# Row 1 of the input and two constant matrices are loaded in 32 by 32 blocks and turned by DVE instead of TensorE

## The reference

```python
rw = softmax(cond_8); w, sel = top_k(rw, 2); w = w / w.sum(-1)     # 8 x 8 logits
# layer 0: two routed experts of eight for each row, and one shared expert
mlp(x, g, u, d) = (gelu(x @ g) * (x @ u)) @ d                      # 256 -> 1024 -> 256
x = x + sum_of_two(w_e * mlp(x, expert_e)) + mlp(x, shared)
# layer 1: a base matrix, and LoRA over 8 experts of rank 16
out  = x @ W_base.T + b_base
lora = einsum('bter,eor,be->bto', x @ As.T, Bs, cond_8)
x = x + out + lora * 2
```

## Time and profile before

| | us |
|---|---|
| median of 3 runs | 806.5 (806.18 to 807.17) |
| the profiled execution | 806.55 |
| its span in the profile | 804.7 |
| outside the span | 1.85 |
| PE busy | 795.9 (99% of the span) |
| DVE busy | 692.3 (86%) |
| ACT busy | 472.3 (59%) |
| POOL busy | 241.2 (30%) |

### The profile page before, as it was taken

The page is one execution under the profiler, slowest core; times in us unless marked ns, Lnnn a source line. Parts: engine busy times, 40 slices in busy tenths (PEclk is TensorE's granted clock), DMA queues, the critical chain, the costliest instruction groups (busy, mean ns, idle before and its releaser), DMA issues.

```text
span 804.7 us, 13013 instructions
## 1 busy us (share of the span) xinstructions
PE 795.9 (99%) x4014; PEld 678.6 (84%) x4014; DVE 692.3 (86%) x896; ACT 472.3 (59%) x715; POOL 241.2 (30%) x218
## 2 busy tenths in 40 slices
PE   9999999999999999999999999999999999999998
PEld 7888888888888888789888889878888887898887
DVE  4886987987876899899989989998898998999886
ACT  5574564554644566476556567556656665765563
POOL 1441321321110443322532412342242332226220
PEclk9999999999999999999999999999999999999999
DMA  7340520303213432353343335235324423623200
GB/s 201 82 118 13 148 76 15 117 1 103 94 40 91 146 118 79 105 157 96 124 140 89 101 119 167 86 104 130 107 96 159 110 79 104 168 96 126 69 1 27
DMA packets 120141, 80.56 MB, mean 100 GB/s; under 512 B 62480, under 2 KB 115472, under 8 KB 120080
## 3 DMA queue, kind: packets, MB, share of 16 engines
q1 hardware_dynamic: 120080, 79.88, 33.0%
HBM read 67.28 MB, written 12.58 MB: 99 GB/s over the span
## 4 chain that ended last, share of the span: by engine, by line
PE 69%; DVE 16%; issue 9%; ACT 2%; POOL 2%; DVEq 1%; DMA 0%; POOLq 0%; ACTq 0%
PE ps_ring L719 42%; PE ps_acc L719 25%; DVE inner_lo L1377 4%; DVE wide L1377 2%; DVE post L1636 2%; DVE post L1696 2%; DVE xc L1377 1%; ACT wide L1048 1%; POOL post L696 1%; DVE post L1611 1%; ACT post L1051 1%; DVE coef_now L1692 1%; DVE post L1654 1%; DVE post L1645 1%; PE ps_ring L839 1%
## 5 line engine op out<-in xcount | busy, mean ns | idle before, releaser
L719 PE MATMUL ps_ring<-xc,wide 128*128 128x512 f32 (+1 forms) x2076 | 454.2, 367 | 0.0
L719 PEld LDWEIGHTS ps_ring<-xc,wide 128*128 128x128 f32 x2076 | 366.3, 188 | 65.6 <-issue 0.2
L1048 ACT CAST inner_hi<-post 128x512 fp32r<-128x512 f32 x192 | 118.1, 623 | 169.6 <-DVE post L1696 87.7
L719 PE MATMUL ps_acc<-inner_hi,wide 128*128 128x512 f32 x504 | 172.9, 391 | 2.4 <-DVE post L1611 2.4
L1377 DVE TENSOR_TENSOR inner_lo<-post,inner_hi 128x512 fp32r<-128x512 f32 x192 | 164.4, 872 | 6.1 <-ACT inner_hi L1048 5.7
L696 POOL TENSOR_TENSOR post<-post 128x512 f32<-128x512 f32 x24 | 31.0, 1292 | 296.5 <-DVE post L1647 296.5
L719 PEld LDWEIGHTS ps_acc<-inner_hi,wide 128*128 128x128 f32 x504 | 94.7, 188 | 24.5 <-issue 4.6
L1051 ACT ACTIVATE post<-ps_ring 128x512 f32<-128x512 f32 (+1 forms) x132 | 73.3, 558 | 54.3 <-PE ps_ring L719 48.1
L719 PE MATMUL ps_acc<-inner_lo,wide 128*128 128x512 f32 x252 | 98.4, 390 | 0.0
L719 PE MATMUL ps_acc<-inner_hi,sh_dn 128*128 128x512 f32 x256 | 83.9, 389 | 0.0
L1696 DVE SCALAR_TENSOR_TENSOR post<-post,coef_now,ps_ring 128x512 f32<-128x512 f32 x80 | 59.5, 744 | 27.8 <-PE ps_ring L719 27.5
(11 more groups left out here) (122 smaller groups left out, 836.6 us busy)
## 6 DMA issues: line engine op xcount, KB each, us to landing
raw<-n_L_cond_skill_gate_dram SPq DMA_DIRECT2D x32, 256.0 KB, 2.7
raw<-in_L_cond_skill_up_dram SPq DMA_DIRECT2D x32, 256.0 KB, 3.3
raw<-n_L_cond_skill_down_dram SPq DMA_DIRECT2D x32, 256.0 KB, 3.7
xbuf<-n_L_cond_skill_gate_dram SPq DMA_DIRECT2D x32, 256.0 KB, 2.8
xbuf<-in_L_cond_skill_up_dram SPq DMA_DIRECT2D x32, 256.0 KB, 3.2
xbuf<-n_L_cond_skill_down_dram SPq DMA_DIRECT2D x32, 256.0 KB, 3.9
xt_scratch<-xbuf SPq DMA_DIRECT2D x8, 512.0 KB, 3.3
sh_scratch<-stage SPq DMA_DIRECT2D x8, 512.0 KB, 2.8
```

Of the source, the lines that this page charges most:

```text
L719: last = pe.matmul(dst, left_[a], right_[b], start=start and n == 0, stop=stop and n == len(PASSES) - 1, skip_group_check=adds)
L1048: return nc.scalar.copy(dst, src)
```

## The change

Row 1 of `x` is loaded in 8 block DMAs in place of one, turned by two DVE transposes straight into `xbuf` (a new semaphore `xt1_in`), and split from there. PE's 8 transposes of row 1 go, and so do ACT's two copies to `xbuf`. `w_base` comes in 8 block DMAs in place of one and B in 8 in place of two; DVE turns both into `w_id` and `b_t` where it copied them out of PSUM. `turn_constants` with its six PE transposes goes.

```diff
@@ SP
+            load_x_blocks(1, x_blk1)
-            sp.dma_start(x_nat1, x_rows[1]).then_inc(x_landed[1], 16)
             load_gate_up(1, sh_landed[1], sh_landed[1])
...
-            sp.wait_ge(turned, 4)
+            sp.wait_ge(xt1_in, 2)
             load_x_blocks(3, x_blk1)
...
+                    w_rows = w_base.rearrange("(k j) h -> j k h", j=32)
                     for c in range(HC):
-                        sp.dma_start(b_nat[:, c, :].rearrange("p (e r) -> p e r", e=E),
-                                     lora_b[:, c * P:(c + 1) * P, :].rearrange("e p r -> p e r"))\
-                            .then_inc(layer1_landed, 16)
-                    sp.dma_start(w_nat, w_base.rearrange("(c p) h -> p c h", p=P))\
-                        .then_inc(layer1_landed, 16)
+                        for g in range(4):
+                            h0 = c * P + 32 * g
+                            sp.dma_start(w_blk[32 * g:32 * (g + 1), c * H:(c + 1) * H]
+                                         .rearrange("j (k i) -> j k i", i=32),
+                                         w_rows[:, :, h0:h0 + 32]).then_inc(layer1_landed, 16)
+                    b_cols = b_blk.rearrange("p (k f r) -> p f k r", f=2, r=R)
+                    for e in range(E):
+                        g, f = divmod(e, 2)
+                        sp.dma_start(b_cols[32 * g:32 * (g + 1), f],
+                                     lora_b[e].rearrange("(k j) r -> j k r", j=32)).then_inc(layer1_landed, 16)
                     store_shared(Q - 1)
@@ PE
-                pe.wait_ge(x_landed[1], 16)
-                for c in range(HC):
-                    turn(acc[1][c], x_nat1, c)
                 pe.wait_ge(left_ready, LEFT_BLOCKS[0])
...
-                    if k == CONST_STEP and first:
-                        pe.wait_ge(acc1_out, 2 * Q)
-                        turn_constants()
                     if k == FOLD_STEP:
                         if first:
-                            pe.wait_ge(w_turned, 1)
+                            pe.wait_ge(acc1_out, 2 * Q)
@@ ACT
             take_xt(0, acc[0][0])
+            act.wait_ge(xt1_in, 1)
+            split_right(0, B12, xt(1, 0))
             gelu_block(0, 0, 0)
+            act.wait_ge(xt1_in, 2)
+            split_right(0, B22, xt(1, 1))
             gelu_block(0, 2, 2)
-            act.wait_ge(turned, 3)
-            split_right(0, B12, acc[1][0][:])
-            act.wait_ge(turned, 4)
-            split_right(0, B22, acc[1][1][:])
             split_left(1)
...
             gelu_block(0, 3, 2)
-            take_xt(2, acc[1][0])
-            take_xt(3, acc[1][1])
@@ DVE
-            split_right(0, B12, acc[1][0][:], 3)
-            split_right(0, B22, acc[1][1][:], 4)
+            dve.wait_ge(x_landed[1], 128)
+            for c in range(HC):
+                V.transpose(xt(1, c), x_blk1[:, c, :]).then_inc(xt1_in, 1)
+            dve.wait_ge(xt1_in, 2)
+            split_right(0, B12, xt(1, 0), 3)
+            split_right(0, B22, xt(1, 1), 4)
...
-                dve.wait_ge(turned_w, 1)
-                V.tensor_copy(b_t[:], ps_misc[1][:, 0:H]).then_inc(b_t_done, 1)
-                V.tensor_copy(w_id[:], ps_misc[0][:]).then_inc(w_turned, 1)
+                dve.wait_ge(layer1_landed, (3 + 2 * E) * 16)
+                V.transpose(b_t[:], b_blk).then_inc(b_t_done, 1)
+                V.transpose(w_id[:], w_blk).then_inc(w_turned, 1)
```

More of the change, by code:

```diff
@@ L153, in cond_resid_kernel @@
         x_nat = xbuf[:, 4 * S:6 * S].rearrange("p (t h) -> p t h", t=TT)
-        x_nat1 = stage[:, 0, :].rearrange("p (t h) -> p t h", t=TT)
         x_blk = xbuf[:, 4 * S:6 * S].rearrange("p (c n) -> p c n", c=HC)
@@ L238, in cond_resid_kernel @@
         a_nat = post[:, 0:H]
-        b_nat = post[:, H:2 * H].rearrange("p (c n) -> p c n", c=HC)
-        w_nat = post[:, 2 * H:4 * H].rearrange("p (c h) -> p c h", c=HC)
+        b_blk = post[:, H:2 * H]
+        w_blk = post[:, 2 * H:4 * H]
         t_tmp = stage[:, 0, :]
@@ L270, in cond_resid_kernel @@
         sum_done = sem("sum_done")
-        turned_w = sem("turned_w")
         fold_done = sem("fold_done")
@@ L277, in cond_resid_kernel @@
         xt0_in = sem("xt0_in")
+        xt1_in = sem("xt1_in")
         right_hi = sem("right_hi")
@@ L441, in store_xt @@
                 if qn == 0:
-                    sp.wait_ge(xt0_in, 2 * r + 2)
+                    sp.wait_ge(xt0_in if r == 0 else xt1_in, 2)
                 else:
@@ L816, in shared_down_part @@
                 if u == 0 and p == 0:
-                    pe.wait_ge(xt0_in, 4)
+                    pe.wait_ge(xt0_in, 2)
                 if q > 0 and j == 0 and p == 0:
@@ L967, in layer1_last @@
                         one(t, 1, 1, 0, False, True).then_inc(l1_done, 1)
[L969 to L977, removed]
             def row(b, par, first):
@@ L1268, in ex_copy_out @@
                     if first:
-                        act.wait_ge(turned_w, 1)
+                        act.wait_ge(w_turned, 1)
                         act.wait_ge(a_ready, 1)
@@ L1354, in row @@
                     if first and k == CONST_STEP:
-                        act.wait_ge(layer1_landed, 6 * 16)
+                        act.wait_ge(layer1_landed, (3 + 2 * E) * 16)
                         take_hi(a_s[0], a_nat).then_inc(a_hi, 1)
@@ L1397, in turn_x @@
             def turn_x(qn, r):
-                dve.wait_ge(x_landed[r], 16 + 128 * qn)
+                dve.wait_ge(x_landed[r], (16 if r == 0 else 128) + 128 * qn)
                 if qn > 1:
```

## The result

| | before | after |
|---|---|---|
| median, us | 806.36 (8 runs, 806.1 to 807.17) | 809.15 (8 runs, 808.52 to 811.32) |
| ratio | | 1.0035 (95% interval 1.0026 to 1.0044) |
| the profiled execution / its span, us | 806.55 / 804.7 | 809.15 / 807.3 |

What follows compares the result with a forecast made beforehand. PE was taken to bound most stretches, but the store, POOL and DVE the second place. Terms -0.68 (start), +0.05 (DVE) and +0.05 (queue) sum to -0.58 us, from 806.55 to 806.0; range 804.9 to 808.3.

Steps and rivals of the forecast that it cites:

- Later SP gains: SP's queue after the start: row 3's blocks issued some 1.7 us earlier, DVE's wait shrinks, 0.10 us comes back.
- the freed wait: SP's second `xt` store no longer waits for ACT's last copy of row 1; through by about 17, not 18.79.
- The rival on the other side: Slower side: sixteen issues hold the shared-result stores back, up to 0.70 us each, 808.1 or more; chance 0.18.
- the second place: Last shared results, stores from about 260 us: PE's transposes worth nothing, DVE 0.05 and queue 0.05 us lost.
- The start's own sum: Start, row 1: 0.88 saved by PE's transposes, less 0.3 stall, plus 0.1 from row 3's blocks, 0.68 us gained.
- The 13.02 of the forecast: Start: when PE asks for all of row 1, from 10.30 plus 12 matmuls of 2.72 us.
- The stall: Start: PE waits some 0.3 us near 13 for row 1's second low part; bounds none to 1.3 us.
- the forecast's 9.85: Start: landing of row 1's blocks, last issue at 7.05 plus 2.8 us, after which DVE transposes.
- rival 2: Start: row 1's blocks land late, after 10.4; at worst PE stalls 4.8 us, time 810.5; chance 0.04.
- 0.6 us forecast here: Start: 0.88 us saved by dropping PE's transposes, less the stall of some 0.3 us.
- the one issue of 2.28 us: Second place: the long issue for `w_base` behind two large loads of B, expected to vanish with smaller loads.

Runs made afterwards that it cites:

- experiment 5: Kernel before, PE's transposes and ACT's copies kept, with seven unneeded block loads of row 1 added behind its one load; 810.07 us, ratio 1.0049.
- experiment 3: Changed kernel with row 3's block loads issued ahead of the third block of shared weights; 807.53 us, ratio 1.001.
- 6: Kernel before with row 3's block loads moved ahead of the third gate, up and down loads; 806.32 us, ratio 0.9997.
- 12: Changed kernel with five of row 1's eight block loads issued by ACT, so that SP issues three; 807.89 us, ratio 1.0017.
- 4: Changed kernel with the two stores of `xt` set apart, one ahead of `load_down(1)`, one behind; 809.69 us, ratio 1.0039.
- experiment 15: Changed kernel, row 3's blocks first, fourteen small DVE fills, ACT casting row 1 before its gelus, POOL's fourth sum later; 805.76 us, ratio 0.9991.
- experiment 8: Kernel before with the constants' part alone, its sixteen loads behind the two stores of the last shared results; 807.06 us, ratio 1.0009.
- experiment 11: Changed kernel with row 3's blocks ahead of the third weights and fourteen small DVE fills at the start; 806.34 us, ratio 0.9997.
- experiment 9: Kernel before with two one-column DVE fills added at the start of the program; 806.73 us, ratio 1.0004.
- experiment 1: Kernel before with only row 1's part of the change, the constants still turned by PE; 810.84 us, ratio 1.0048.

## Why the prediction was wrong

**The step that failed is SP's queue in the first 30 us.** It read "Later SP gains" and had row 3's blocks issued 1.7 us earlier, for a gain of 0.1 us in the sum; they were issued to the end 1.5 us later, PE waited 1.63 us for what hangs on them, and the 24 matmuls then took 5.72 us, not 5.44. The issue times were nearly right (8 loads in 5.97 us, 5.6 forecast) and the freed wait was right. What was left out is that a transfer that may start sooner competes with others: the seven more loads set the second weights back by 5.5 us and row 2's blocks by 2.7, the wait in which the DMA engines had emptied was gone, and the third weights, two stores and row 3's blocks met. Experiments 5 (more loads alone bring it), 3 with 6 (the order alone takes it away, and gains nothing in the kernel before), 12 (a shorter queue of SP takes it away with the same bytes, and with the freed wait) and 4 (not the neighbouring stores alone) show it. Its price is 1.6 us by the medians. The earlier trace rows already said that PE was 0.1 us from waiting there: no later landing was free.

**The rival on the other side** put the held-back queue at the second place, at the stores of the shared results, from 0.54 us an issue. There the sixteen took 0.54 each as forecast. It was the right mechanism at the wrong place; that the change made SP's queue longer at two places was seen, but only one was given a bad case.

**The start's own sum**: 0.88 us saved was right. PE's demand came at 12.72. The 13.02 of the forecast took PE's start from the timeline (10.30) and its pace from the chain, where the same start is 10.47; the chain alone gives 13.19, and this execution was 0.44 us earlier from its first gate matmuls on (7.02 for 7.46). The stall was 0.72, not 0.3 but inside its bounds of 0 to 1.3. DVE began at 10.25, 0.4 us after the forecast's 9.85 but before the 10.4 from which rival 2 counts; the low parts took 0.83 us each on average (0.9 was taken for the second). The row of 60 matmuls, 13.64 us without a stop, became 2.73 and 11.17, 0.26 more: a break in PE's stream costs something beside the wait. It costs it for the shortest break too (11.22 us in experiment 15, behind a stop of 0.02 us). Of 0.6 us forecast here nothing was left. Some of the stall is only PE's early arrival: in the profiled run of experiment 3 it came to these matmuls at 10.67, did not stop, took 13.64 us for the 60, and was through at 24.31, 0.3 us ahead of the changed kernel. Experiment 15 shows the sum as it was meant: from 806.34 to 805.76 when the stall goes.

**The second place**: PE's transposes were worth nothing, as said, since PE still waited 1.4 us there. DVE's transposes cost what the copies did (0.66 for 0.68). Of the one issue of 2.28 us little was left (the eight of `w_base` took 4.65 us, the eight of B 3.90). The misses are the first store, 0.30 us late, and the landing of the second, 0.70 us slower, with 0.45 given back by POOL; experiment 8 did not show its cause.

**What no step had**: 0.9 us in the profile, 1.2 by the medians of experiments 3 and 11, from where DVE's instructions lie. In these runs it goes with the number of instructions ahead of the loop over rows. The exact rule is open: the kernel before with two small operations (experiment 9) lost nothing, the changed one with its two transposes did, so waits or another engine's instructions count as well. What DVE waits for in these gaps no row shows; that it is the loading of its instructions is a guess. The Trainium skill (Advanced Engine Details and Errata, ISA Cache) describes a cache for instructions of only two lines; no run here shows a cache or a size.

By medians, then: 805.76 in experiment 15, plus 0.6 for the stall, plus 1.2 for the place of DVE's instructions (experiment 11 against 3), plus 1.6 for the queue (experiment 3): 809.15. These steps add up by the way they are formed, and they cross chips. Set against its own runs of the kernel before, each kernel lies at -0.9, -0.4, +1.0 and +2.8 us, which makes the steps 0.5, 1.4 and 1.8. The forecast had -0.6 for what experiment 15 reached with two repairs and fourteen fills.

## What to carry to other kernels

When a change puts more DMAs into a queue, follow every load behind them to its consumer, and ask at each one what else is then under way; a wait that goes away may have been what kept the DMA engines free. Give each place where a queue gets longer its own bad case, above all where PE has only 0.1 us to spare. In a kernel with a long loop measure a change of some tenths of a percent also with a few empty instructions ahead of the loop: here they moved the time by up to 2.4 us.

## What was unexpected of the hardware

- DVE idles by itself at some places of a loop, 0.33 us in rows 2, 4 and 6 or 0.9 to 1.4 us in rows 3 and 5, as the number of instructions before the loop changes.
- Behind a wait of PE of 2.0 us (experiment 1) the granted clock stood at 0.50, the 1.2 GHz level, for some 3 us; a longer wait of 2.7 us in the profiled run of experiment 5 left it at 1.00. This makes the price of such a wait uneven: 809.4 or 812.8 for one kernel.
- The price of a low part depends on when it falls: 1.77 us beside POOL's sums, 0.68 without.
